# A two-layer language-model tower with routed experts: four normalisations move from VectorE to ScalarE, the order of work on every engine is written anew, and the resident experts are counted earlier

## The reference

```python
h = take(table, x)                                    # L0_tok
h = h + attn0(layernorm(h))                           # causal linear attention, 16 heads of 16, elu+1 features
h = h + (layernorm(h) @ CB.T) * (SCB / 127) + bias    # L0_ffn
h = h + attn1(layernorm(h))                           # 64 random softmax features a head; stab of k = max over a
                                                      # head's tokens and features; +residual, layernorm, relu
                                                      # MLP 256-1024-256, layernorm
z = layernorm(h)
h = h + onehot(argmax(z @ router)) . expert_e(z * sigmoid(top logit)) + shared_expert(z)   # 8 experts, gated 256-512-256
```

## Time and profile before

| | us |
|---|---|
| median of 3 runs | 688.7 (688.22 to 689.7) |
| the profiled execution: its time | 687.8 |
| its span | 686.0 |
| PE busy in the span | 619.5 (90%) |
| DVE busy | 492.1 (72%) |
| ACT busy | 285.8 (42%) |
| POOL busy | 254.0 (37%) |
| mean granted clock of TensorE | 0.973 |

### The profile page before, as it was taken

One profiled execution on the slowest core, in us unless ns is written; L12 is line 12 of the kernel. 1 busy time (PEld: TensorE's weight loads), 2 busy tenths in 40 slices (PEclk: granted clock), 3 DMA queues, 4 the chain that ended last, 5 costly groups with the idle time before them and its releaser, 6 DMA issues.

```text
span 686.0 us, 15421 instructions
## 1 busy us (share of the span) xinstructions
PE 619.5 (90%) x5960; PEld 500.2 (73%) x5960; DVE 492.1 (72%) x1171; ACT 285.8 (42%) x687; POOL 254.0 (37%) x405
## 2 busy tenths in 40 slices
PE   5878799998999999999999999999993079999997
PEld 4657588887888978898888988989992035555563
DVE  3998999999999988999989988976574012322322
ACT  2345566565465545546454454554320011222221
POOL 5443334435425342442524325312313014435433
PEclk9998999999999999999999999999998579999999
DMA  7950000000000000000000000000012861152550
GB/s 258 415 239 10 1 10 10 1 17 10 10 9 10 24 2 16 10 9 10 10 17 1 17 10 17 10 16 17 16 39 56 324 242 55 61 210 77 226 212 29
DMA packets 17367, 46.85 MB, mean 68 GB/s; under 512 B 6913, under 2 KB 11536, under 8 KB 14864
## 3 DMA queue, kind: packets, MB, share of 16 engines
q1 hardware_dynamic: 13136, 37.47, 14.4%
q0 software_dynamic: 4160, 8.41, 3.9%
HBM read 40.54 MB, written 6.89 MB: 69 GB/s over the span
## 4 chain that ended last, share of the span: by engine, by line
PE 65%; DVE 20%; issue 5%; ACT 3%; SPq 3%; DMA 2%; POOL 0%; another core or an unknown queue 0%; POOLq 0%; DVEq 0%; ACTq 0%
PE ps L1133 61%; DVE stats L716 3%; PE ps L1138 2%; DVE H_S L775 2%; DVE rdenTA L798 1%; SPq L318 1%; PE ps L1290 1%; SPq L317 1%; DVE qf L888 1%; DVE rdenTB L909 1%; ACT qkA L694 1%; DMA home_rows<-send_home 1%; DVE mv L717 1%; DVE x L732 1%; DVE H_S L732 1%
## 5 line engine op out<-in xcount | busy, mean ns | idle before, releaser
L415 POOL TENSOR_TENSOR var_eps<-mv,ln_eps 128x1 f32<-128x1 f32 x112 | 24.3, 217 | 280.2 <-DVE mv L717 275.4
L1133 PE MATMUL ps<-yTC,we 128*128 128x128 f32 x1024 | 123.1, 276 | 0.0
L1133 PEld LDWEIGHTS ps<-yTC,we 128*128 128x128 f32 x1024 | 120.0, 193 | 1.3 <-issue 0.2
L1133 PE MATMUL ps<-we,yTA 128*128 128x256 f32 (+1 forms) x272 | 89.3, 464 | 31.1 <-SPq L376 28.8
L1133 PEld LDWEIGHTS ps<-we,yTA 128*128 128x128 f32 x272 | 50.2, 198 | 52.9 <-issue 49.0
L416 POOL TENSOR_TENSOR rstd<-var_eps,pow_half 128x1 f32<-128x1 f32 x112 | 63.9, 570 | 8.8
L1133 PE MATMUL ps<-we,ffT 128*128 128x256 f32 x256 | 60.8, 380 | 0.0
L1133 PE MATMUL ps<-we,yTB 128*128 128x256 f32 (+1 forms) x176 | 54.8, 440 | 0.0
L1133 PEld LDWEIGHTS ps<-we,ffT 128*128 128x128 f32 x256 | 47.2, 190 | 6.9
L1133 PEld LDWEIGHTS ps<-we,yTB 128*128 128x128 f32 x176 | 32.2, 191 | 13.8 <-issue 11.5
L775 DVE TENSOR_TENSOR H_S<-ps,causal_sb 128x512 f32<-128x512 f32 x64 | 39.9, 677 | 2.0 <-PE ps L1133 2.0
(11 more groups left out here) (216 smaller groups left out, 1331.6 us busy)
## 6 DMA issues: line engine op xcount, KB each, us to landing
we<-w_experts SPq DMA_DIRECT2D x8, 1536.0 KB, 13.9
H_S<-w_experts SPq DMA_DIRECT2D x8, 1536.0 KB, 9.7
we<-w_ff SPq DMA_DIRECT2D x2, 1024.0 KB, 9.1
x_rows<-send_x SPq DMA_DIRECT2D x16, 128.0 KB, 1.7
home_rows<-send_home SPq DMA_DIRECT2D x16, 128.0 KB, 2.1
rows_sb<-rows SPq DMA_DIRECT2D x1, 1664.0 KB, 6.3
we<-w_qk SPq DMA_DIRECT2D x2, 512.0 KB, 4.5
we<-w_v SPq DMA_DIRECT2D x2, 256.0 KB, 4.7
```

Of the source, the lines that this page charges most:

```text
L415: link(pool.tensor_tensor(var_eps[:, k:k + 1], mv[:, k, 1:2], ln_eps[:], ALU.add))
L1133: return pe.matmul(o, a, b, start=start, stop=stop)
```

## The change

- `normalise` for k = 0, 2, 3, 6 is an ACT instruction (Identity with scale `rstd` and bias `centre_at` = -mean * rstd). POOL computes `centre_at` with two more 128x1 operations after the power.
- The orders and lags of all five queues are new, and so are the PSUM banks and the `after` waits that guard them. PE's lags go to 12 and DVE's to 13: `c_ga` 9 to 11, `c_up` 10 to 11, `c_dn` 11 to 12, `c_f1`, `c_f2` 6 to 7, `a_v`, `a_num`, `a_out`, `a_ffn`, `b_ctx`, `b_out`, `c_T5` one later. On ACT only differences of lags mean anything, since all its lags are shifted.
- SP raises `experts_ready` to 1 in `ids0`, in the tower, and to 2 and 3 as soon as experts 4 and 5 have landed, ahead of `load_halves(0)`; `load_ids(5)` comes last.
- The maximum of k is spread with 128 rows (`one_all` x `km_diag` with zero rows) in place of 16.

```diff
-        km_diag = sb("km_diag", [HEADS, HEADS])
-        one16 = sb("one16", [HEADS, P])
+        km_diag = sb("km_diag", [P, HEADS])
+        one_all = sb("one_all", [P, P])
 # SP
             def ids0(t):
                 if t == T - 1:
+                    sp.wait_ge(S["residents_loaded"], 16 * RESIDENT)
+                    sp.sem_inc(S["experts_ready"], 1)
                     sp.wait_ge(S["table_ready"], 1)
                     sp.wait_ge(S["ids_scattered"], 16 * T)
                     load_ids(0)
-                (1, ids0), (10, ids3), (4, ids1), (0, x_out), (8, ids2), (2, home_out),
+                (4, home_out), (0, x_out), (9, ids2), (3, ids1), (9, ids3), (1, ids0),
             load_late(RESIDENT)
             load_late(RESIDENT + 1)
             load_ids(4)
             load_late(RESIDENT + 2)
             load_late(RESIDENT + 3)
+            late_is_ready(RESIDENT)
+            late_is_ready(RESIDENT + 1)
             sp.wait_ge(S["tile_done"], T)
             sp.wait_ge(S["table_ready"], 2)
             load_halves(0)
+            late_is_ready(RESIDENT + 2)
+            late_is_ready(RESIDENT + 3)
             load_ids(5)
-            sp.wait_ge(S["residents_loaded"], 16 * RESIDENT)
-            sp.sem_inc(S["experts_ready"], 1)
-            for e in range(RESIDENT, E):
-                sp.wait_ge(late_loaded[e], 16)
-                sp.sem_inc(S["experts_ready"], 1)
 # POOL
+            def deviation_and_centre(k, t):                       # k = 0, 2, 3, 6
+                link(inverse_deviation(k, t))
+                link(pool.tensor_tensor(centre_at[:, k:k + 1], mv[:, k, 0:1], rstd[:, k:k + 1], ALU.mult))
+                pool.tensor_tensor(centre_at[:, k:k + 1], centre_at[:, k:k + 1], minus_one[:], ALU.mult
+                                   ).then_inc(S[f"centre{k}_ready"], 1)
-                (2, gat), (6, pA2), (8, r4), (5, pA), (7, pB), (6, r3), (11, scat), (7, hC), (9, r5), (5, r1),
-                (1, r0), (5, r2), (8, pC), (9, r6),
+                (8, r4), (6, pA2), (7, pB), (5, pA), (6, r3), (5, r1), (1, gat), (9, r5), (5, r2), (8, pC), (0, r0),
+                (7, hC), (11, scat), (9, r6),
 # ACT
+            def normalise(dst, src, k, t):                        # a_norm, a_norm2, b_norm, c_norm
+                act.wait_ge(S[f"centre{k}_ready"], t + 1)
+                return act.activation(dst, src, ACT.Identity, bias=centre_at[:, k:k + 1], scale=rstd[:, k:k + 1])
-                (4, b_yT), (1, a_par), (6, c_yT), (5, b_rqT), (0, a_yT), (5, b_cx2), (4, b_x), (4, b_sq), (0, a_x),
-                (4, b_dgc), (4, b_rk), (6, c_ra), (3, a_yT2), (6, c_rb), (4, b_eq), (8, c_send), (0, a_exp),
-                (4, b_ek), (7, c_yT2), (4, b_keps), (9, c_th), (4, b_cT), (7, c_tt), (1, a_rd),
+                (7, b_norm), (8, b_cT), (7, b_yT), (11, c_yT2), (4, a_par), (8, b_cx2), (5, a_rd), (9, c_yT),
+                (7, b_x), (7, b_sq), (6, a_norm2), (3, a_x), (7, b_dgc), (7, b_rk), (9, c_ra), (11, c_tt), (6, a_yT2),
+                (3, a_exp), (9, c_rb), (2, a_yT), (7, b_eq), (1, a_norm), (13, c_th), (7, b_ek), (7, b_keps),
+                (11, c_send), (7, b_rqT), (10, c_norm),
 # DVE: a_norm, a_norm2, b_norm, c_norm are gone
+                (9, c_o), (0, a_stats), (5, a_res), (7, b_cx), (3, a_vz), (11, table0), (4, a_rec), (3, a_m3),
+                (3, a_m2), (4, a_mean), (3, a_m1), (3, a_m0), (13, c_hid), (11, table1), (7, b_rec), (10, c_log),
+                (7, b_mean), (6, b_dgr), (6, b_km), (6, b_qs), (9, c_res), (6, kmx), (10, c_choose), (7, b_o),
+                (6, b_ks), (6, b_vo), (11, table2), (12, c_gc), (7, b_x1), (5, a_ff), (2, a_max), (10, c_slot),
+                (12, table3), (13, c_down), (4, a_o), (2, a_elu),
 # PE
-                matmul(kb[:, 0:HEADS], one16[:], km_diag[:], True, True).then_inc(S["kmax_psum"], 1)
+                matmul(kb[:, 0:HEADS], one_all[:], km_diag[:], True, True).then_inc(S["kmax_psum"], 1)
-                (2, a_den), (4, b_T3), (0, a_T0), (5, b_qT), (4, b_qk), (5, b_cTT), (1, a_s), (11, c_dn), (0, a_qk),
-                (5, b_h), (4, b_dg), (4, b_kq), (4, b_dgT), (6, c_fa), (6, c_fb), (3, a_T2), (5, b_out), (4, b_kmT),
-                (6, c_f1), (4, b_v), (4, b_kmB), (10, c_up), (8, c_cn), (3, a_ffn), (6, c_f2), (7, c_T6), (2, a_out),
-                (9, c_ga), (0, a_v), (7, c_lo), (5, c_T5), (1, a_num), (4, b_ctx),
+                (6, b_out), (1, a_v), (11, c_ga), (0, a_T0), (5, b_kmB), (4, a_ffn), (7, c_f1), (12, c_dn),
+                (3, a_out), (9, c_cn), (5, b_qT), (7, c_f2), (2, a_num), (5, b_ctx), (2, a_den), (4, b_T3), (8, c_T6),
+                (6, c_T5), (5, b_cTT), (4, b_qk), (1, a_s), (0, a_qk), (11, c_up), (5, b_h), (4, b_dg), (4, b_kq),
+                (8, c_lo), (4, b_dgT), (6, c_fa), (3, a_T2), (6, c_fb), (4, b_kmT), (4, b_v),
```

More of the change, by code:

```diff
@@ L1164, in a_qk @@
                 pe.wait_ge(S["src0T_ready"], t + 1)
+                after(pe, "ctx_even", t - 4)
+                after(pe, "ctx_odd", t - 4)
                 by_channel(qk0, yTA, qk0_sb, range(4)).then_inc(S["qk0_psum"], 1)
@@ L1177, in a_s @@
                 pe.wait_ge(S["qz_ready"], t * 2 + 2)
-                after(pe, "qT_ready", t - 3)
+                after(pe, "src5T_ready", t - 4)
+                after(pe, "ff2_read", t - 5)
                 for half in range(2):
@@ L1189, in a_num @@
                 pe.wait_ge(S["scores_masked"], t * 4 + 4)
+                after(pe, "tile_done", t - 9)
                 for half in range(2):
@@ L1258, in b_dgT @@
                 pe.wait_ge(S["diagT_out"], t + 1)
+                after(pe, "hT_ready", t - 6)
                 pe.transpose(dg[:, 0:P], dgT_sb[:], id_sb[:]).then_inc(S["diag_psum"], 1)
@@ L1281, in b_kq @@
                     after(pe, "scores_masked", (t + 3) * 4 + 3)
-                after(pe, "tile_done", t - 6)
+                if t + 4 < T:
+                    after(pe, "x_ready", (t + 4) * 4 + 4)
                 features(D, KD)
@@ L1287, in b_qT @@
                 pe.wait_ge(S["qfeat_ready"], t + 1)
-                after(pe, "logit_copied", t - 2)
+                after(pe, "kexp_in", t + 1)
+                after(pe, "gC_ready", t - 5)
                 for pair in range(PAIRS):
@@ L1296, in b_ctx @@
                 pe.wait_ge(S["v1_ready"], t + 1)
-                after(pe, "ff2_read", t - 1)
+                if t + 1 < T:
+                    after(pe, "ffn0_read", t + 2)
                 for i in range(4):
@@ L1331, in c_T5 @@
                 pe.wait_ge(S["x1_ready"], t + 1)
+                after(pe, "counts_read", t - 2)
                 transposed(T5, x1).then_inc(S["src5T_psum"], 1)
@@ L1337, in c_fa @@
                 pe.wait_ge(S["src5T_ready"], t + 1)
+                if t + 5 < T:
+                    after(pe, "scores_masked", (t + 5) * 4 + 4)
                 by_channel(fa, yTC, ff1_sb, range(4)).then_inc(S["ffa_psum"], 1)
@@ L1354, in c_f1 @@
                 pe.wait_ge(S["ffa_ready"], t * 4 + 4)
+                if t + 7 < T:
+                    after(pe, "src0T_ready", t + 8)
                 second_layer(t, 0)
@@ L1362, in c_T6 @@
                 pe.wait_ge(S["src6_ready"], t + 1)
+                if t + 5 < T:
+                    after(pe, "out0_read", t + 6)
                 transposed(T6, yC).then_inc(S["src6T_psum"], 1)
@@ L1372, in c_ga @@
                 pe.wait_ge(S["src6T_ready"], t + 1)
+                if t + 6 < T:
+                    after(pe, "qexp_in", (t + 6) * 2 + 2)
                 after(pe, "gC_ready", t)
@@ L1377, in c_up @@
                 pe.wait_ge(S["src6T_ready"], t + 1)
+                if t + 10 < T:
+                    after(pe, "v0_ready", t + 11)
                 by_channel(up, yTC2[t % AHEAD], su_sb, range(KE)).then_inc(S["up_psum"], 1)
@@ L1382, in c_cn @@
                 pe.wait_ge(S["onehot_ready"], t + 1)
+                if t + 4 < T:
+                    after(pe, "v1_ready", t + 5)
                 matmul(cn[:, 0:E], before16[:], onehot[:], True, True)
```

135 lines of the change are left out of this document (66 added, 69 removed).

## The result

| | before | after |
|---|---|---|
| median, us | 689.2 | 658.9 (654.3 to 660.3, 4 runs) |
| ratio to before | | 0.954, 95% interval 0.949 to 0.960 |
| profiled execution: time, span | 687.8, 686.0 | 657.5, 655.7 |
| mean granted clock | 0.973 | 0.994 |

The kernel is 4.6% faster. The forecast was 650.5 us, range 640 to 666: the direction came out, and so did the mechanism of the largest term, and the gain is some 8 us short in this measurement. The changed kernel was measured twice more, on other occasions: 654.6 us (ratio 0.948, 0.945 to 0.951) and 655.4 us (0.951, 0.949 to 0.954).

The account below looks back on a forecast made before the run. PE was taken to bound 200 to 515 us, DVE with PE 60 to 200, and SP's late increment a 28.8 us hole. Span 686.0 - 28.4 - 1.8 + 1.5 - 1.3 - 8.0 = 648.0, told as median 650.5, range 640 to 666.

Parts of the forecast that it names:

- The hole: Between tower and experts: SP's increment moved forward lets round 0 start once x is there; gain 28.4 us.
- The warm first round: Expert round 0: after a pause of only a few us PE's clock stays at 2.4 GHz; gain 1.8 us.
- Rounds 0 to 2: First expert rounds: stores, home and x gathers slowed by weight loads beside them; loss 1.5 us, bounds 0 and 8.
- The tail: Last `slot_u` to x: later lags leave more PE work to cover the gap; gain 1.3 us, bounds -1.5 and +4.
- The tower: Tower stage: DVE sheds normalisations where it binds, from 60 to 200 us; gain 8 us, at most 24, loss at most 11.
- My test for DVE: Sign of a right forecast: DVE's busy share from 60 to 200 us falls below 0.9.
- (1): Tower gains nothing or loses a little, extra iteration and longer chain cancelling DVE's relief: 658 to 664 us; chance 0.22.
- (2): Expert rounds 0 to 2 held up by weight loads, x or home late, up to 8 us: 657 us; chance 0.10.
- (3): Steady part from 200 to 400 us also faster by denser weight loads, 7 us: 643; chance 0.12 with more tower gain.
- (4): Early increment doesn't start PE; table, ids or home rows hold it until loads are through: 680 us; chance 0.02.
- (5): Each normalisation over three queues makes PE wait, some 5 us an iteration; slower than before, 730 us; chance 0.04.

Follow-up runs that it names:

- a0_changed: The changed kernel unaltered, measured again on another occasion: 654.6 us, ratio 0.948 to the kernel before.
- a1_changed: The changed kernel unaltered, measured once more on another occasion: 655.4 us, ratio 0.951 to the kernel before.
- e1: The kernel before with only SP's early `experts_ready` increments, its own orders and normalisations kept: 664.4 us, ratio 0.961.
- e3: e1 with the four normalisations on ScalarE (centres by POOL) in the old orders, `b_norm` behind `a_rd`: 696.6 us, ratio 1.007.
- e3b: e3 with `b_norm` and `a_norm` moved ahead of `a_rd` in ScalarE's list: 682.2 us, ratio 0.990.
- e4: The changed kernel with the maxima of k spread by 16 rows again: 659.9 us, ratio 0.957.
- e5: The changed kernel's orders with the four normalisations back on VectorE, `b_norm` behind `c_o`: 692.4 us, ratio 1.003.
- e5b: e5 with `b_norm` first in VectorE's list, ahead of `c_o`: 679.1 us, ratio 0.982.
- e6: The changed kernel with late experts loaded and counted in the order 7, 6, 5, 4: 657.5 us, ratio 0.952.
- e7: The changed kernel with PE's four register loads of round 0 ahead of the transposes of the first x: 656.0 us, ratio 0.951.
- e9: The changed kernel with late experts in order 7, 6, 5, 4, register loads ahead and two home-row buffers: 649.9 us, ratio 0.944.
- e10: e9 with unread matmuls of ones in PE's pauses at the start and near the tower's end: 649.4 us, ratio 0.943.

## Why the prediction was right, and where it was not

The forecast's gain in span, part by part, and what the profiles gave, in us:

| | forecast | first profile | a0_changed | a1_changed |
|---|---|---|---|---|
| tower, to the last `slot_u` | 8.0 | 5.1 | 7.8 | 7.8 |
| from there to x of round 0 in SBUF | 1.3 | -0.2 | 0.8 | 0.0 |
| from x to round 0 | 28.4 | 26.3 | 26.1 | 26.1 |
| expert part (warm round and rounds 0 to 2) | 0.3 | -0.9 | -1.4 | -1.4 |
| sum | 38.0 | 30.3 | 33.3 | 32.6 |

The largest term carries the forecast. Every term came out below its forecast.

**The hole (forecast 28.4 us).** Right in mechanism and place; 26.0 us in e1. What I took for "late next" was x, at 525.3. Behind x stood PE's own four register loads, 2.6 us. They were there before, hidden under the 28.8 us wait, and no row of the trace before shows them. That is the missing term.

**The warm first round (1.8 us).** 14.44 became 12.63 us in the first profile, by luck. Ten profiles have the register loads between x and round 0, the changed kernel's three and those of e1, e3, e3b, e4, e5, e5b and e6. In nine of them the clock fell to 1.2 GHz near the start of round 0, and the round took 14.0 to 15.7 us, so the term was wrong as a rule. A pause of 2.4 to 2.8 us, behind waits for x, went with it each time. With the loads moved away (e7, e9, e10) the round took 12.6 us in all three.

**Rounds 0 to 2 (1.5 us lost, bounds 0 and 8).** The size was near, by luck: rounds 0 to 2 last 40.2 us, where three unhindered ones are 37.9, so 2.3 are lost. The reason was not. I assumed evenly spread tokens and no need of a late expert before round 4. Whole tiles 0 to 4 are expert 2's and 5 to 14 are expert 7's, the last of the four to be loaded, so tile 5 in round 2 waits for it. No wait of PE for x or for a silu is over 0.3 us in these rounds of the first profile, so late stores stopped it nowhere. The halves were issued 24.6 us after the last `c_dn` (forecast 20.6 and 1 or 2 more) and landed, with the loads beside them, 13.8 us later:

```profile
we<-w_experts SPq DMA_DIRECT2D x2, 1536.0 KB, 14.4
H_S<-w_experts SPq DMA_DIRECT2D x2, 1536.0 KB, 13.8
```

From 538.55 to 557.8 four loads are 4.8 us each, against the 4.4 from the earlier trace rows; PE wanted the halves at 566, so the forecast that they would be in time held.

**The tail (1.3 us gained).** From `slot_u` to x in SBUF 18.1 us, where 17.9 were: nothing gained (17.1 and 17.9 in the repeats). This step failed in the first profile by one number: I bounded the landing of the home rows by 2.5 us, from a store of results. Issued 0.4 us after the scatter of 128 ids it took over 8 us, DVE stood 3.5 us in `c_down`, and PE 2.4 us in `c_dn`. That is no rule. In a0_changed, a1_changed, e4, e6 and e7, where the same store followed the scatter by 0.1 to 0.4 us, `c_down` of tile 13 didn't wait for it. There DVE waited in `c_down` of tile 14, for the store of tile 13 that stands behind ids0 in SP's queue, which is the order of things that the prediction described. In a0_changed:

```profile
507.11 2.03 SPq L319 DMA_DIRECT2D ids<-sorted_ids  x2
509.19 2.82 SPq L308 DMA_DIRECT2D home_rows<-send_home  x2
511.23 0.42 DVE L1104 TENSOR_TENSOR send_home<-ps,H_S 128x256 f32<-128x256 f32 x1 [1.38 <-DMA home_rows<-send_home]
```

The waits there are 1.1 to 2.5 us, inside the bound of 3. From `slot_u` to the end of the last `c_dn` are 17.1 us in the first profile, 14.7 and 15.4 in the repeats, and 14.5 in e9_all, where `c_down` waits for no store. And ids0 follows the last scatter by 6.8 to 8.5 us in every profile (7.8 in the kernel before), which no second buffer helps.

**The tower (8.0 us gained).** `slot_u` of the last tile came 5.1 us earlier in the first profile and 7.8 in the two repeats. The size held, and so did the shape: in a0_changed the first maxima of k come 3.1 us later than before (54.7 against 51.6 us), the eight periods behind them (to 255 us there) are 13.1 us shorter, and the last seven are 0.7 us shorter. Part of the 13.1 is 1.2 GHz in the first period of the trace before (the clock fell there at 52 us). The attribution didn't hold. I gave it all to DVE's relief between 60 and 200 us and nothing to the spread of maxima. Some 3 to 4.5 us are the spread (e4_rows16), which leaves about as much for orders and normalisations together; which of the two it is stays open. How far one profile can be trusted here: e1, with the tower of the kernel before, has its last `slot_u` at 509.0 us against 507.4. My test for DVE, a share below 0.9 from 60 to 200 us, came out at 0.93. And the full period did not stay: it is 30.07 us, not 29.9. The spread gives 0.3 us back in each, and other neighbours cost more than that. One of them is `b_qk` (L1150, yTB), which lasts 2.17 us to the next start now that the 32-row `a_s` follows it, and lasted 1.79 before a transposition.

**The rivals.** (1) was the nearest to the first measurement (658), though the tower did gain. Of the 7.7 us that the first profile fell short, 2.9 were in the tower, 1.5 from `slot_u` to x, 2.1 before round 0 and 1.2 in the expert part. (2) came small, with 2.3 us, and for a late expert, not for late stores. (3), a faster steady part, failed: PE's weight loads from 200 to 400 us rose only from 175.3 to 177.6 us. With it falls the reading of weight-load density as a reserve. (4) did not come, save for the 2.6 us. (5) did not come in the changed kernel (1.3 us of waits for yB, 1.1 for yA), but in e3 it did, with 30.8. e5 has a wait of the same kind (28.8 us) with the normalisations on VectorE, so it is the place in a list that makes it and not the engine alone. The rival's chance of 0.04 rested on where the stages stand in the lists, not on the rows of before.

## What to carry to other kernels

Where a long wait is taken away, list all that the waiting engine itself does behind it, its register loads too: a long wait hides them, and they are next. Ask of the data, not of the average, which weights are wanted first. And in a pipeline whose orders are fixed by hand, a stage moved to another engine is worth what its place in the list makes of it: the same move was 14 us apart with two stages placed otherwise. Few rows in a matmul saved nothing where TensorE was full: the change of one small matmul's shape was worth 3 to 4.5 us. And before an explanation is drawn from one profile, look whether its wait is there in a second profile of the same kernel: the store of 8 us and the wait for expert 7 each stood in one of the changed kernel's three.

## What the runs showed of the hardware

- Four register loads on PE (two tiles' expert and needed value) took 2.4 to 2.8 us ahead of round 0 in ten profiles, and nothing that is seen when they stood ahead of the transposes of x.
- A matmul on 16 rows between matmuls on 128 took longer than the same one filled up with rows of zeros: the transposition ahead 0.31 us to the next start in place of 0.22, the pair itself 0.32 in place of 0.14 (e4_rows16 against a1_changed).
- SP's first load of the ids, which waits for the last scatter of 128 ids, came 6.8 to 8.5 us after that scatter's issue in fourteen profiles. A store of 128 KB issued 0.4 us after that scatter freed its buffer only after 8 us in one profile; in five others, where it was issued 0.1 to 0.4 us after, it was free when DVE wanted it, 5.0 to 5.2 us after its issue.
- Where TensorE's clock falls to 1.2 GHz differs between executions of one kernel. Where PE paused 2.4 to 2.8 us for its register loads before round 0, behind one or two waits for x, it fell in nine profiles of ten. The tenth, the first profile of the changed kernel, has no wait for x there. In e7, e9 and e10, where the pauses at that place are under 1 us each, it did not fall.
